# Layer norm moved from GpSimd to VectorE, together with six small moves in the order of work, in a fused attention and mixture-of-experts block

## The chip, the cores and the metric

The kernel runs on one core of a Trainium2 chip. The time is device microseconds of one execution. Before the change the median of three runs is 666.53 us (665.94 to 667.35).

## What is computed

```
x: (4, 512, 256)   ctx: (4, 1024, 192)   16 heads of 16, 8 experts, hidden 1024
x = x + tanh(g_xattn) * xattn(layernorm(x), ctx)
    q, k, v = linear(...)                        # with biases
    attn = softmax(clip(q k^T / 4, +-10000));    out = (attn v) @ Wo + bo
x = x + tanh(g_ffn) * ffn(layernorm(x))
    n = layernorm(x) * rsqrt(mean square + 1e-8) * norm_weight
    shared = relu(n @ sw1 + sb1) @ sw2 + sb2
    top 2 of 8 experts by sigmoid(n @ router^T), their weights made to sum to 1
    routed = sum over the two experts of weight * (relu(n @ ew1[e] + eb1[e]) @ ew2[e] + eb2[e])
    ffn = shared + routed
```

All tensors are fp32. Products keep fp32 accuracy by splitting each operand in a high and a low part and adding three matmuls (high-high, high-low, low-high).

## The kernel before, in words

Every engine has its own instruction list, and the lists meet at semaphores, so an instruction that waits holds up all that stands behind it on its engine. There are three stages.

**Preparation** (0 to 85 us). For each of the four batches n the list PREP (L388) gives the order of small steps, the same on TensorE (PE), ScalarE (ACT) and VectorE (DVE): TC, context transposes; K, Q, V, projections with halves or tiles j; TX, two transposes of the layer-normed x; N, checks on norms. In the batches 0 to 2 the second half of a batch is K2, K3, N0, V0, V1, N1, TX0, V2, TX1, V3; the last batch has the two TX ahead of K2. Eight PSUM banks are used in turn, so PE's step f waits for the DVE's step f-8. A batch's Q is made after the next batch's TC. ACT makes the high part of a step and DVE the low part. K and Q go out to DRAM through five stage buffers, and come back stacked by head: SP, the DMA queue, writes out step s and then starts up to three of batch 0's stack loads (L553 and the loop below it). The layer norm of batch n has three parts: statistics on DVE (`ln_x_stats`, L1096, at the step STATS_AT, just ahead of V2), the reciprocal root on GpSimd (POOL) and the subtract-and-scale of four tiles of 128 x 256, also on POOL (both in `norm_x`, L776). TX waits for it through the semaphore xn_done. The split of the weight wo is one DVE job (SPLIT_AT, L1318), ahead of TC0 of batch 1.

**Attention** (85 to 330 us). PE makes scores, ACT exponentials, PE the products with v in bank pv; DVE transposes each group's result out of pv and signals pv_read.

**Feed forward** (from 330 us), `feed_forward` on PE, ACT and DVE. The work is a list of chunks: chunks 0 to 4 are the shared expert on 256 tokens each; then 21 routed chunks in the order FFHFFFHFFHFFFHFFHFFHF, F of two tiles of tokens and H of one; then three shared ones. Each chunk has eight slots q: for two tiles PE does h0 to h3 (hidden layer, chunk i) and r0 to r3 (second layer of chunk i-1); for one tile the order is h0 h1 r0 h2 r1 h3 r2 r3, so that r0 of the chunk before comes after only two h. PE transposes the next chunk's input in slot `turn_at(i)` (L458), and DVE splits it there (`split_x`). ACT, at slot 0, first converts the next set's first weight (`w1_high`, 1 MB), and only then makes this chunk's relus, in order; DVE makes the low parts: `w1_low`, `split_h`(q) after each relu pair, `w2_low` at slot 6. A relu pair q waits for `split_h`(q-2), because its buffers are two. `w2_low` must end before r0 of this chunk, which stands in the next chunk. For an F chunk w1_low is in slot 0, but in slot 2 when the next chunk is H (there are six such places).

The last batch's remaining attention steps are put in between the shared chunks by LAST_AT (in eighths of a chunk, for PE) and LAST_READ (for DVE): the router's logits and top two at 18 on PE and 17 on DVE (`post`, `top_two`), the places of the tokens at 20 (`places`), which ends in the tile dest. POOL then scatters the rows of the tokens to slot_x in DRAM, and SP loads them by expert (`load_slot`). SP's list after that is written out by hand (L700): slot 0, w1(2), slot 1, biases(1), w2(1), then a loop over slot, w1, w2 and biases.

Of the kernel before, what the change touches and what calls it, by code (L numbers as in the profile page):

```python
# [27 lines left out]
def flamingo_block(nc, x, ctx_kv, g_xattn, g_ffn, wq, bq, wk, bk, wv, bv, wo, bo,  # L28
# [77 lines left out]
    with ExitStack() as top:  # L106
# [297 lines left out]
        FILLS = len(PREP)  # L404
        STATS_AT = (V, 2)
        STAGED = [(n, kind, j) for n, kind, j in PREP if kind in (Q, K)]
# [46 lines left out]
        X, EIGHTHS = "x", 8  # L453
        LAST_AT, LAST_READ = [3, 4, 16, 16, 18, 20], [3, 4, 16, 16, 17, 20]
        ZEROS_AT, LAST_NORM, SLOTS_AT = 10, 12, (20, 21)
        COMBINE_AT = [EIGHTHS * (AHEAD + MAIN) + k for k in COMBINE_E]

        def turn_at(i):  # L458

            return 6 if i == AHEAD - 1 else 4 if one_tile(i) else 2 if i == 0 or one_tile(i - 1) else 3  # L460

# [70 lines left out]
        def _(sp):  # L532
# [167 lines left out]
            load_slot(0)  # L700
            load_w1(2)
            load_slot(1)
            load_biases(1)
            load_w2(1)
            for j in range(MAIN):
                if j + 2 < MAIN:
                    load_slot(j + 2)
                if j + 3 < SETS:
                    load_w1(j + 3)
                load_w2(j + 2)  # L710
                load_biases(j + 2)
# [40 lines left out]
        def _(pool):  # L752
# [23 lines left out]
            def norm_x(n):  # L776
                wait_stats()
                rsqrt(0, mv[:, 0, :, 1], LN_EPS).then_inc(rstd_done, 1)
                pool.wait_ge(rstd_done, rounds[0])
                for t in range(QT):  # L780
                    last = nc.gpsimd.tensor_scalar(normed[:, n * QT + t, 0:D], x_sb[:, n * QT + t, :], mv[:, 0, t, 0:1],
                                                   rs[:, 0, t:t + 1], ALU.subtract, ALU.mult)
                    if t < QT - 1:
                        step(last)
                last.then_inc(xn_done, 1)

# [273 lines left out]
        def _(dve):  # L1060
# [35 lines left out]
            def ln_x_stats(n):  # L1096
                dve.wait_ge(loaded_x[n], 16)
                if n:
                    dve.wait_ge(xn_done, n)
                for t in range(QT):  # L1100
# [3 lines left out]
                last.then_inc(stats_done, 1)  # L1104
                stat_rounds[0] += 1

            def prep(f):
# [209 lines left out]

            SPLIT_AT = {(0, TC, 0): (W_K, wk_p), (0, K, 0): (W_V, wv_p), (0, K, 1): (W_Q, wq_p), (1, TC, 0): (W_O, wo_p)}  # L1318
            dve.wait_ge(ident_set, 1)
# [4 lines left out]
            for f, (n, kind, j) in enumerate(PREP):  # L1324
# [26 lines left out]
                if (n, kind, j) == (0, TC, 0):  # L1351
                    dve.wait_ge(loaded_bias, 80)
                    v.tensor_copy(bias_rows[0:2 * KD, :].rearrange("k (d q) -> k d q", q=PH),
                                  qk_rows[:, :].rearrange("k (q d) -> k d q", q=PH)).then_inc(bias_sorted, 1)
                if n + 1 < B and (kind, j) == STATS_AT:
                    ln_x_stats(n + 1)
# [253 lines left out]
            for i in range(len(CHUNKS)):  # L1610
                s = set_of(i)
                for q in range(EIGHTHS):
# [7 lines left out]
                    if at_e == LAST_NORM:  # L1620
                        norm_mlp(B - 1)
                    for k, when in enumerate(LAST_READ):
                        if when == at_e:
# [6 lines left out]
                    if q == turn_at(i) and i + 1 < len(CHUNKS):  # L1630
                        split_x(i + 1)
                    if CHUNKS[i][0] == F and q == (2 if one_tile(i + 1) else 0):
                        w1_low(s + 1)
# [54 lines left out]
        def _(pe):  # L1688
# [245 lines left out]
            def results(i, e):  # L1934

                s = set_of(i)
                if e == 0:
                    pe.wait_ge(w2_lo, s + 1)
                    pe.wait_ge(h_split, (i + 1) * HM // 2)
                    if i == 0:  # L1940
                        pe.wait_ge(pv_read, B * GROUPS)
                    if i >= 2:
# [15 lines left out]
            def feed_forward():  # L1958

                for i in range(len(CHUNKS)):  # L1960
                    for q in range(EIGHTHS):
# [71 lines left out]
```

## Time and profile before

| | us |
|---|---|
| median of the three runs | 666.53 |
| the profiled execution's own time | 665.94 |
| its span, first to last instruction | 664.2 |
| PE busy | 635.5 (96%) |
| ACT busy | 529.5 (80%) |
| DVE busy | 414.5 (62%) |
| POOL busy | 152.5 (23%) |

The span is 1.7 us shorter than the execution's own time. The page's PE count comes from modelled ends of pipelined matmuls, so that a busy PE is a PE with work in it, and its idle time is read from the gaps in the order of time. Times in the rows are in us from the span's start unless they are marked ns.

### The profile page before, as it was taken

Reading aid. Unit: us, or ns where it says so; the run is one execution under the profiler, and the core shown is the slowest. Engines: PE = TensorE matmul, PEld = TensorE weight load, DVE = VectorE, ACT = ScalarE, POOL = GpSimd, SP = SyncE. Lnnn points to the kernel's source line nnn. Section 1 sums busy time; section 2 is a strip of 40 time slices with the busy share of each in tenths; the row PEclk is TensorE's granted clock in tenths of the full one; section 3 lists DMA queues with packets and bytes.
Section 4 is the critical chain, followed back from the end, with each engine's and each line's share of the span. In section 5 each row is a group of like instructions: output and inputs, shape, how many; then the busy total and the mean of one; then the engine's idle time right before and its main releaser. Section 6 shows DMA issues by size and latency. Waiting matters only on the chain.

```text
span 664.2 us, 13111 instructions
## 1 busy us (share of the span) xinstructions
PE 635.5 (96%) x4733; PEld 451.1 (68%) x4733; DVE 414.5 (62%) x764; ACT 529.5 (80%) x852; POOL 152.5 (23%) x177
## 2 busy tenths in 40 slices
PE   5899989999999999999999999999999999999995
PEld 4678722223333323333399989999999999999995
DVE  5888710103434243434778867888797888888776
ACT  4577669999999899999873479687989979798850
POOL 3744260000403110410150400232222212314100
PEclk9999979999999999999999999999999999999998
DMA  7999900938398774943020896778878787894083
GB/s 249 301 327 287 376 20 1 130 53 104 78 237 160 131 91 54 121 91 124 10 64 1 195 299 223 250 235 256 259 245 285 240 257 249 259 284 161 29 277 125
DMA packets 75221, 118.52 MB, mean 178 GB/s; under 512 B 10933, under 2 KB 55945, under 8 KB 73993
## 3 DMA queue, kind: packets, MB, share of 16 engines
q1 hardware_dynamic: 66640, 102.38, 56.6%
q0 software_dynamic: 4416, 13.13, 7.0%
q10 hardware_dynamic: 4088, 2.05, 1.2%
q8 instruction: 41, 0.67, 0.5%
q14 instruction: 36, 0.29, 0.2%
HBM read 86.01 MB, written 31.52 MB: 177 GB/s over the span
## 4 chain that ended last, share of the span: by engine, by line
PE 49%; DVE 16%; ACT 12%; DMA 10%; issue 7%; POOL 2%; SPq 1%; ACTq 0%; POOLq 0%; DVEq 0%
PE pv L1824 19%; PE sc L1790 14%; PE sc L1695 5%; DMA b_sb<-in_L_ffn_eb 3%; ACT h_f L1018 3%; ACT h_p L1021 3%; ACT w_p L972 3%; DVE h_p L1546 3%; DVE w_p L1415 3%; PE pv L1950 2%; PE sc L1950 2%; DVE x_sb L1602 2%; PE mb L1695 2%; ACT w_p L978 2%; DMA slot_x<-second,dest 1%
## 5 line engine op out<-in xcount | busy, mean ns | idle before, releaser
L988 ACT ACTIVATE prob<-sc 128x1024 f32<-128x1024 f32 x172 | 169.2, 1180 | 11.5 <-PE sc L1790 11.5
L1018 ACT ACTIVATE h_f<-sc,b_sb 128x256 f32<-128x256 f32 (+1 forms) x232 | 94.0, 481 | 64.8 <-issue 22.6
L1695 PE MATMUL sc<-xt_p,w_p 128*128 128x256 f32 x1104 | 140.8, 284 | 2.6 <-DVE xt_p L1077 1.1
L1695 PEld LDWEIGHTS sc<-xt_p,w_p 128*128 128x128 f32 x1104 | 133.5, 190 | 5.7 <-DVE xt_p L1077 4.3
L1790 PEld LDWEIGHTS sc<-q_stack,k_stack 48*128 48x128 f32 x512 | 45.3, 186 | 114.0 <-ACT prob L988 62.4
L1790 PE MATMUL sc<-q_stack,k_stack 48*128 48x512 f32 x512 | 106.8, 476 | 2.9 <-ACT prob L988 2.2
L860 POOL DMA_INDIRECT y_tok<-y_sb,y_row x36 | 58.1, 1613 | 196.4 <-DVE y_sb L1566 191.8
L1021 ACT ACTIVATE h_p<-sc,b_sb 128x256 fp32r<-128x256 f32 (+1 forms) x232 | 95.4, 499 | 0.0
L1824 PE MATMUL pv<-prob,v 128*17 128x512 f32 x688 | 92.1, 608 | 0.2
L1546 DVE TENSOR_TENSOR h_p<-h_f,h_p 128x512 fp32r<-128x512 f32 x104 | 70.6, 687 | 34.2 <-ACT h_p L1021 34.1
L988 ACT ACTIVATE clip<-sc 128x1024 f32<-128x1024 f32 x84 | 88.0, 1183 | 1.7 <-PE sc L1790 1.7
L1950 PE MATMUL pv<-w_p,h_p 128*128 128x256 f32 x624 | 78.8, 284 | 0.3 <-issue 0.3
L1950 PE MATMUL sc<-w_p,h_p 128*128 128x256 f32 x624 | 78.2, 282 | 0.0
L1950 PEld LDWEIGHTS pv<-w_p,h_p 128*128 128x128 f32 x624 | 76.3, 191 | 0.8 <-issue 0.5
L1950 PEld LDWEIGHTS sc<-w_p,h_p 128*128 128x128 f32 x624 | 75.5, 189 | 0.5 <-DVE w_p L1420 0.4
L1375 DVE STREAM_TRANSPOSE o_q<-pv 128x512 f32<-128x512 f32 x16 | 11.5, 717 | 98.7 <-PE pv L1824 98.7
L1420 DVE TENSOR_TENSOR w_p<-w_raw,w_p 128x2048 fp32r<-128x2048 f32 x23 | 52.7, 2291 | 15.7 <-ACT w_p L978 15.7
L1415 DVE TENSOR_TENSOR w_p<-w_raw,w_p 128x2048 fp32r<-128x2048 f32 x23 | 52.7, 2289 | 1.9 <-ACT w_p L972 1.6
L972 ACT ACTIVATE w_p<-w_raw 128x2048 fp32r<-128x2048 f32 x22 | 43.0, 1955 | 11.0 <-DMA b_sb<-in_L_ffn_eb 10.4
L1824 PE MATMUL pv<-clip,v 128*17 128x512 f32 x336 | 44.2, 598 | 0.1
L978 ACT ACTIVATE w_p<-w_raw 128x2048 fp32r<-128x2048 f32 x22 | 43.8, 1991 | 0.0
L872 POOL DMA_INDIRECT slot_x<-normed,dest x16 | 16.4, 1028 | 115.6 <-DVE dest L1243 111.9
(271 smaller groups left out, 674.8 us busy)
## 6 DMA issues: line engine op xcount, KB each, us to landing
w_raw<-in_L_ffn_ew SPq DMA_DIRECT2D x42, 1024.0 KB, 6.5
k_stack<-k_rows SPq DMA_DIRECT2D x36, 256.0 KB, 10.4
k_rows<-stage_p SPq DMA_DIRECT2D x24, 256.0 KB, 4.4
q_stack<-q_rows SPq DMA_DIRECT2D x36, 128.0 KB, 11.5
y_tok<-zero_t POOLq DMA_DIRECT2D x8, 512.0 KB, 20.9
w_raw<-in_L_ffn_sw SPq DMA_DIRECT2D x4, 1024.0 KB, 7.6
y_all<-y_tok SPq DMA_DIRECT2D x8, 512.0 KB, 8.7
x_in<-slot_x SPq DMA_DIRECT2D x15, 257.0 KB, 2.8
```

The source lines that it names most:

```text
L860: pool.indirect_dma_start(out=y_tok, out_offset=bass.IndirectOffsetOnAxis(ap=y_row[i % 4][:, t:t + 1], axis=0), in_=y_sb[i % 2][:, t, :], ...
L972: nc.scalar.activation(w1_p[s % 2][0][:, :, :], w1_raw[s % 3], ACT.Copy).then_inc(w1_hi, 1)
L978: nc.scalar.activation(w2_p[s % 2][0][:, :, :], w2_raw[s % 2], ACT.Copy).then_inc(w2_hi, 1)
L988: nc.scalar.activation(prob_3[w % 3][u % 2][:, :, :], sc[u % 3][:, :, :], ACT.Exp, scale=SCALE).then_inc(exp_done, 1)
L1018: last = nc.scalar.activation(copy[:, m % len(ms), :], src[:, m % len(ms), :], ACT.Relu, bias=b1_sb[s % 3][:, m:m + 1])
L1021: last = nc.scalar.activation(high[:, m, :], src[:, m % len(ms), :], ACT.Relu, bias=b1_sb[s % 3][:, m:m + 1])
L1415: v.tensor_tensor(w1_p[s % 2][1][:, :, :], w1_raw[s % 3], w1_p[s % 2][0][:, :, :].bitcast(F32), ALU.subtract).then_inc(w1_lo, 1)
L1546: v.tensor_tensor(lo, src, hi.bitcast(F32), ALU.subtract).then_inc(h_split, 1)
L1695: last = mm(dst, lhs(a, k), rhs(b, k), start=(i == 0), stop=(i == len(todo) - 1))
L1790: return mm(dst[:, a, :], k_stack[rows, 2 * g + i, kt * P:(kt + 1) * P], q_stack[rows, 2 * g + i, :], start=True, stop=True)
L1824: last = mm(pv[32 * j:32 * j + DH + 1, :], v_sb[b][:, kt, HEADS // 2 * (j % 2) + 2 * g + j // 2, :], probs[w % len(probs)][j // 2][:, j % ...
L1950: last = mm(result_of(i, t), h_p[i % 2][a][:, k, t * P:(t + 1) * P], w2_p[s % 2][b][:, k, :], start=((k, a, b) == (0, 0, 0)), stop=((k, a, ...
```

## The change

The subtract-and-scale of the first layer norm goes from POOL to DVE as `ln_x`, ahead of K2 (of K0 in the last batch). The statistics come one step later, ahead of V3. The split of wo comes ahead of K3 of batch 0. DVE's logits step goes to 18, as on PE. slot_counts and slots go one eighth later. Chunk 4's turn of the next input goes from slot 6 to 5. SP's order after slot 0 becomes biases(1), w2(1), slot 1, w1(2). w1_low of every F chunk is in slot 0. PE waits for the last pv_read ahead of the first feed-forward product instead of ahead of the first second-layer product.

```diff
-        STATS_AT = (V, 2)
+        LN_AT, LN_LAST, STATS_AT = (K, 2), (K, 0), (V, 3)
-        LAST_AT, LAST_READ = [3, 4, 16, 16, 18, 20], [3, 4, 16, 16, 17, 20]
-        ZEROS_AT, LAST_NORM, SLOTS_AT = 10, 12, (20, 21)
+        LAST_AT = [3, 4, 16, 16, 18, 20]
+        ZEROS_AT, LAST_NORM, SLOTS_AT = 10, 12, (21, 22)
         def turn_at(i):
-            return 6 if i == AHEAD - 1 else 4 if one_tile(i) else 2 if i == 0 or one_tile(i - 1) else 3
+            return 5 if i == AHEAD - 1 else 4 if one_tile(i) else 2 if i == 0 or one_tile(i - 1) else 3
             load_slot(0)
-            load_w1(2)
-            load_slot(1)
             load_biases(1)
             load_w2(1)
+            load_slot(1)
+            load_w1(2)
                 # POOL, norm_x(n)
                 pool.wait_ge(rstd_done, rounds[0])
-                for t in range(QT):
-                    last = nc.gpsimd.tensor_scalar(normed[:, n * QT + t, 0:D], x_sb[:, n * QT + t, :], mv[:, 0, t, 0:1],
-                                                   rs[:, 0, t:t + 1], ALU.subtract, ALU.mult)
-                    if t < QT - 1:
-                        step(last)
-                last.then_inc(xn_done, 1)
                 # DVE, ln_x_stats(n)
-                if n:
-                    dve.wait_ge(xn_done, n)
+            def ln_x(n):
+                dve.wait_ge(rstd_done, stat_rounds[0])
+                for t in range(QT):
+                    last = v.tensor_scalar(normed[:, n * QT + t, 0:D], x_sb[:, n * QT + t, :], mv[:, 0, t, 0:1],
+                                           rs[:, 0, t:t + 1], ALU.subtract, ALU.mult)
+                    if t < QT - 1:
+                        step(last)
+                last.then_inc(xn_done, 1)
-            SPLIT_AT = {..., (1, TC, 0): (W_O, wo_p)}
+            SPLIT_AT = {..., (0, K, 3): (W_O, wo_p)}
+                if (kind, j) == (LN_LAST if n == B - 1 else LN_AT):
+                    ln_x(n)
-                    for k, when in enumerate(LAST_READ):
+                    for k, when in enumerate(LAST_AT):
-                    if CHUNKS[i][0] == F and q == (2 if one_tile(i + 1) else 0):
+                    if q == 0 and CHUNKS[i][0] == F:
                         w1_low(s + 1)
                 # PE, results(i, e)
-                    if i == 0:
-                        pe.wait_ge(pv_read, B * GROUPS)
             def feed_forward():
+                pe.wait_ge(pv_read, B * GROUPS)
```

## Rows read from the trace of the kernel before

**Rows 1.** Busy time by stretch: stretch, its length, busy time and count of each engine, clock, DMA.
```profile
0.00:86.00 86.00, 72.55 (x419) 60.55 (x419) 66.83 (x134) 50.31 (x86) 37.18 (x65) 1.00 0.90 299
...
460.00:627.00 167.00, 165.03 (x1331) 160.41 (x1330) 137.84 (x158) 143.32 (x287) 43.53 (x27) 1.00 0.73 234
```
**Rows 2.** Timeline, batch 0's layer norm: start, length, engine, line, operation, [idle before <- releaser].
```profile
19.64 5.20 POOL L781 TENSOR_SCALAR normed<-x_sb,mv,rs 128x256 f32<-128x256 f32 x4
...
24.98 0.63 PE L1721 MATMUL sc<-ident,normed 128*128 128x128 f32 x4 [2.65 <-POOL normed L781]
```
**Rows 3.** Timeline, the same operation on DVE in the second layer norm.
```profile
349.76 1.38 DVE L1309 TENSOR_SCALAR normed<-x_sb,mv,rs 128x256 f32<-128x256 f32 x4
```
**Rows 4.** DMA issues of 15.25 to 15.5 us (the last of wo): count, size, landing.
```profile
w_raw<-in_L_xattn_Wo SPq DMA_DIRECT2D x2, 32.0 KB, 8.3
```
**Rows 5.** Timeline of DVE, the split of wo.
```profile
30.79 0.42 DVE L1075 CAST wo_p<-w_raw 128x512 fp32r<-128x512 f32 x1
...
31.24 0.69 DVE L1077 TENSOR_TENSOR wo_p<-w_raw,wo_p 128x512 fp32r<-128x512 f32 x1
```
**Rows 6.** Timeline of DVE, SP and ACT in the batches 2 and 3.
```profile
57.54 0.75 DVE L1135 SCALAR_TENSOR_TENSOR stage_p<-sc,qk_col,stage_p 128x512 fp32r<-128x512 f32 x1 [0.40 <-ACT stage_p L948]
...
67.93 1.20 SPq L566 DMA_DIRECT2D q_rows<-stage_p  x2
...
78.70 0.69 ACT L947 ACTIVATE stage_s<-sc,qk_col 128x512 fp32r<-128x512 f32 x1 [0.75 <-DMA k_rows<-stage_p]
```
**Rows 7.** Timeline, start of the feed-forward stage.
```profile
330.38 3.14 PE L1695 MATMUL sc<-xt_p,w_p 128*128 128x256 f32 x24
...
330.51 0.72 DVE L1375 STREAM_TRANSPOSE o_q<-pv 128x512 f32<-128x512 f32 x1 [0.20 <-PE pv L1824]
...
334.41 0.84 ACT L1018 ACTIVATE h_f<-sc,b_sb 128x256 f32<-128x256 f32 x2 [5.47 <-DMA b_sb<-in_L_ffn_sb]
```
**Rows 8.** Timeline of DVE from the logits to the places.
```profile
357.74 0.31 DVE L1187 STREAM_TRANSPOSE logits<-sc 128x128 f32<-128x128 f32 x1
...
360.78 1.28 DVE L1546 TENSOR_TENSOR h_p<-h_f,h_p 128x512 fp32r<-128x512 f32 x2
...
366.22 0.17 DVE L1243 CAST dest<-dest_f 128x8 uint32<-128x8 f32 x1
```
**Rows 9.** Chain of waits, the first routed input: start, length, what.
```profile
385.64 2.65 DMA x_in<-slot_x
```
**Rows 10.** Timeline of PE, first products of chunks 5 and 6.
```profile
392.93 4.48 PE L1695 MATMUL sc<-xt_p,w_p 128*128 128x256 f32 x36 [1.01 <-issue]
...
404.82 4.48 PE L1695 MATMUL sc<-xt_p,w_p 128*128 128x256 f32 x36
```
**Rows 11.** Timeline of SP, the load of w2(1).
```profile
390.70 0.38 SPq L662 DMA_DIRECT2D w_raw<-in_L_ffn_ew  x1
```
**Rows 12.** DMA issues of 390.6 to 391.1 us.
```profile
w_raw<-in_L_ffn_ew SPq DMA_DIRECT2D x1, 1024.0 KB, 5.9
```
**Rows 13.** Timeline of ACT, DVE and PE, chunks 5 to 7.
```profile
393.64 1.92 ACT L972 ACTIVATE w_p<-w_raw 128x2048 fp32r<-128x2048 f32 x1 [4.33 <-DMA b_sb<-in_L_ffn_eb]
...
415.86 2.28 DVE L1420 TENSOR_TENSOR w_p<-w_raw,w_p 128x2048 fp32r<-128x2048 f32 x1
...
419.21 1.60 PE L1950 MATMUL pv<-w_p,h_p 128*128 128x256 f32 x12
```
**Rows 14.** Timeline of DVE, ACT and PE, chunk 13 and the H chunk behind it.
```profile
484.76 0.69 DVE L1546 TENSOR_TENSOR h_p<-h_f,h_p 128x512 fp32r<-128x512 f32 x1 [0.70 <-ACT h_p L1021]
...
485.89 0.96 ACT L1018 ACTIVATE h_f<-sc,b_sb 128x256 f32<-128x256 f32 x2
...
491.01 2.28 DVE L1420 TENSOR_TENSOR w_p<-w_raw,w_p 128x2048 fp32r<-128x2048 f32 x1
...
493.40 1.63 PE L1950 MATMUL sc<-w_p,h_p 128*128 128x256 f32 x12
```
**Rows 15.** Timeline of ACT, an F chunk whose w1_low is in slot 0.
```profile
444.02 0.84 ACT L1018 ACTIVATE h_f<-sc,b_sb 128x256 f32<-128x256 f32 x2 [0.97 <-DVE h_p L1546]
```

More of the change, by code:

```diff
@@ L1314, in norm_mlp @@
                                 ALU.mult).then_inc(normed_done, 1)
-            SPLIT_AT = {(0, TC, 0): (W_K, wk_p), (0, K, 0): (W_V, wv_p), (0, K, 1): (W_Q, wq_p), (1, TC, 0): (W_O, wo_p)}
+            SPLIT_AT = {(0, TC, 0): (W_K, wk_p), (0, K, 0): (W_V, wv_p), (0, K, 1): (W_Q, wq_p), (0, K, 3): (W_O, wo_p)}
             dve.wait_ge(ident_set, 1)
```

## The prediction, made before the changed kernel was run

> **What bounds the kernel.** I read the busy time by stretch first, then the order of time of each engine at every place that the diff touches, then the waits and the DMA landings there. In the routed part PE works 165 of 167 us, so what makes PE late there is seldom given back; DVE has 138 and ACT 143 us of work in the same 167, in strict order, and so the question at each place is whether a moved step comes too late for PE. In the preparation DVE has 67 of 86 us and PE 73 [rows 1]. The attention stage in between is passed through whole: a shift at its start is a shift at its end.
>
> **Layer norm on DVE.** POOL takes 5.2 us for the four tiles, and PE stood idle 2.65 us for them in batch 0 [rows 2]. DVE takes 1.38 us for the same four in the second layer norm [rows 3]. Ahead of K2 of batch 0 DVE would end it near 21.2, so the PE wait of rows 2 goes. What is late next is DVE itself. The last piece of wo, issued at 15.4, lands 8.3 us later, at 23.7 [rows 4], while DVE is now at its split before K3, near 21.9: it waits 1.8 us, and the split takes 0.42 + 0.69 = 1.1 [rows 5]. K3, N0, V0, V1, N1 and TX0 queue behind it, and so PE's banks. I get DVE's split of TX1, for which Q waits, at 29.9 instead of 30.3, and then the statistics (2.2 us, now behind it) make the splits of the next TC about 0.9 later than before. ACT, which is full at K0 and K1 of batch 1, takes that up. So the gain of 2.65 is gone by batch 1.
>
> In the batches 1 and 2 the 1.38 us comes on DVE between K1 and K2, where it waited 0.40 for ACT before each K [rows 6]; two such gaps hide 0.8 and 0.6 stays. TX1 comes earlier than before in its batch, since the statistics are behind it, and spares PE short waits for Q, but the TC splits after it are 0.6 later, and with them Q of batch 2, whose write holds SP. SP starts that pair of writes at 67.93 and issues back to back from there up to the write of K0 [rows 6]; ACT waits at 78.70 for the landing of that write. All later steps to the first scores hang on it: **+0.6 us**. The bounds: -2.3 if wo costs nothing and the earlier Q is kept by PE, +1.5 if DVE's whole 1.38 counts. I take 0.6 as what the order of time gives. The x tiles wanted by bo come no later. On POOL only the copies of ctx follow, and they come earlier.
>
> The Trainium skill speaks against the move ("Perfetto Trace Analysis", Optimizing Scalar/DVE Operations): with DVE saturated, moving work off it, even to GPSIMD, may make sense. The trace agrees only in part, with 67 of 86 us. By that rule alone, an estimate with the duration of the rows, 1.38 us would be paid in full in each of the three later batches, 4.1 us instead of 0.6.
> It also says where the two meet ("SBUF — State Buffer", Who interferes with whom): VectorE and GpSimd share one port pair, and whoever comes second blocks for the whole instruction; a tensor_scalar from SBUF to SBUF can take the pair. No row of the kernel before shows this operation beside a POOL copy. By that rule the copies of ctx, which now follow the root at once, could hold back ln_x in two batches; one block would be under a microsecond, and it is in no term of the sum.
>
> **Wait for pv_read ahead of feed_forward.** PE starts the first product at 330.38, DVE's last transposition runs 330.51 to 331.23 [rows 7]. PE starts 0.9 later, and h0 to h3 and the two wo steps are queued behind. But ACT's first relu waits for the biases until 334.41 [rows 7], with h0 ready at 332 before and 333 now, and PE waited later on for a split of DVE's that hangs on that relu. **0**, and 0.9 if this cover were gone.
>
> **Logits on DVE at 18.** At 17 DVE took the logits at 357.74 and did chunk 2's second and third split_h together at 360.78, 3.0 us later [rows 8]. Now the second split comes first. Its relus end near 358.5, the split takes 0.7, so the logits start at 359.2, 1.5 later. PE's places wait for the masks 2.4 us on, 361.7 instead of 360.75: PE stands 1.0. On DVE one split fewer follows, so that dest, at 366.22 before, comes 1.0 later. From dest the path goes through POOL's eight scatters to the first routed input, landing at 388.3 [rows 9]. **+1.0**, bounds 0 and 1.5. The shift of slot_counts and slots changes no neighbour on DVE (there is nothing in those slots of chunk 2): 0.
>
> **Turn of the first routed input in slot 5.** PE gets to it after r0, waits until 389.3 for the landing, and has 0.4 of transposes and r1 to r3, 36 matmuls in 4.3 us, to do after it: 394.1. Before, chunk 5 began at 392.93, with 1.0 of waiting for w1_low [rows 10]. Against 393.9 by the last step alone, **+0.2**, bounds 0 and 1.5 (r1 alone).
>
> **SP's order.** The new place of w1(2) is the issue at 390.7, which was w2(1)'s and landed 5.9 us later, at 396.6, with the same bytes ahead of it [rows 11, 12]. ACT waited until 393.64 (for the biases, which were behind w1(2)) [rows 13]. It converts w1(2) before it makes a relu of chunk 5, so it starts 3.0 later; w1_low, the splits and the input of chunk 6 queue behind it. With the 1.0 of above: w1_high ends 399.6, w1_low 401.9, the first split 402.5, the third relu pair 404.0, its split 404.6, the input's split 406.1. PE wants it at 404.82 + 1.2 = 406.0 [rows 10]. So +0.2 there. ACT then runs relus, w2(1) and w1(3) to 409.2. DVE has w2_low (409.6), two steps of read_y (411.0), w1_low(3) (413.3), two splits, the input, the expert weights (419.3), w2_low (421.6). It began this last one at 415.86 and ended it 1.07 us ahead of PE's r0 at 419.21 [rows 13]. PE now wants it at 420.6 and waits 1.0. **+1.2**, bounds -0.3 (the biases come early) and +3.0 (all of it).
>
> **w1_low in slot 0 before an H chunk.** Its 2.29 us now stands ahead of the first split_h, for which ACT's third relu pair waits. Where that order is in the trace already, ACT idles 0.97 us for the split [rows 15]. At chunk 13 DVE is free at 484.06, waits 0.70 for ACT and splits at 484.76, and ACT's third pair begins at 485.89 unhindered [rows 14]. Now: w1_low to 486.3, split to 487.0, third pair 1.1 later, and so w2_high; w2_low, which began at 491.01 as soon as DVE was free, begins near 491.8 and ends at 494.1. PE began r0 at 493.40, with only the two h of an H chunk as cover [rows 14]: +0.7. Of six such places three are like this (I work out 0.7, 0.85 and 0.6); in the other three w2_low ends 1 us or more ahead of r0, as in rows 13. **+2.2**, bounds -0.4 (the input's split comes earlier) and six times 1.1, 6.6.
>
> **Sum.** 0.6 + 1.0 + 0.2 + 1.2 + 2.2 = 5.2. On the profiled execution's own 665.94 (span 664.2 and 1.7 around it) that is **671.1**. That execution is 0.6 below the median of the three, so by the median it would be 671.7; I keep 671.1.
>
> **Rivals.**
> *The stretch before the scores decides (faster).* PE's 2.65 us wait goes and is not replaced: wo has landed or its split is hidden, Q of batch 0 starts 2.3 earlier and all to the end is carried along; the other edits fall into slack. For it: POOL's chain is on the chain of waits there. Against it: 8.3 us to landing [rows 4]. It decides if DVE's TX1 split of batch 0 ends before 28.5. Time 665.9 - 2.3 = 663.6. Chance 0.1.
> *Only the dispatch counts.* The losses in routed chunks fall on waits that PE has anyway, or earlier input splits give them back: 0.6 + 1.2 = 1.8, 667.7. For it: PE idles about 2 us in that part [rows 1]. Against it: r0 behind an H's two h has no cover. Chance 0.2.
> *Every H place pays.* Three more at 0.9: 5.2 + 2.7, 673.8. For it: later w2_low holds back SP's next load. Against it: slack of rows 13. Chance 0.1.
> *The forecast*: 0.6, its own range 668.5 to 673.5.
>
> **Numbers.** The range 666.8 to 674.2 leaves out the faster case and a little at the top. Taking 0.2% (1.3 us, about what a measurement of this kernel can tell from no change) around 666.5: the faster case gives 0.1, the second case half its 0.2 for no change, the rest slower: 0.1, 0.1, 0.8.
>
> **What would show it.** In the profile after: DVE idle or waiting for wo at about 22 to 24; no PE wait for normed in batch 0, and first scores 0.6 later; dest 1.0 later relative to the last product with v; ACT waiting for a w_raw load near 397; ACT idle for split_h in the third pair of the chunks before H; PE waiting for w2_low ahead of r0 in H chunks. The forecast fails if the first scores come 2 us earlier, or if w2_low of chunks 13, 20 and 23 still ends ahead of r0.

## The result, and the profile of the changed kernel

The changed kernel takes 675.1 us (median of 4, 673.48 to 675.87), the kernel before beside it 666.94 us: a ratio of 1.0116, 95% interval 1.0088 to 1.0145, 8 us slower. The forecast of 671.1 us (666.8 to 674.2) had the sign and missed the size. A later set of runs of both gave 1.0086 (1.0056 to 1.0116).

The profiled execution of the changed kernel takes 674.95 us; its span is 673.2 us, where that of the kernel before was 664.2. I lay the same PE instructions of both traces side by side. How much later than before:

| place | changed kernel later by, us | forecast |
|---|---|---|
| first score | 2.32 | 0.6 |
| turn of the first routed input | 3.31 | 1.6 |
| turn in chunk 5 (second routed input) | 3.51 | 1.8 |
| turn in chunk 6 | 5.56 | 2.0 |
| turn in the first H chunk | 6.45 | 3.0 |
| last routed input | 9.11 | 5.2 |

By these offsets the preparation lost 2.3 us (forecast 0.6), the dispatch and the turn 1.2 (1.2), SP's order 2.9 (1.2), and w1_low in slot 0 2.7 (2.2).

Stretches of the changed kernel, columns as in [rows 1]:
```profile
0.00:86.00 86.00, 71.27 (x411) 60.01 (x411) 69.16 (x143) 50.45 (x86) 16.69 (x48) 0.96 0.90 299
...
460.00:627.00 167.00, 162.89 (x1307) 157.72 (x1306) 136.33 (x157) 140.23 (x280) 55.49 (x28) 1.00 0.75 243
```
The norm left POOL (37.2 to 16.7 us in the first 86). DVE has only 2.3 us more in these 86, because the stage is longer now; up to the first score of each kernel it has 69.7 us where it had 65.3. The last column but two is the granted clock: 0.96 in place of 1.00 in the preparation.

DVE in batch 0, the place of [rows 2, 4, 5]:
```profile
19.90 1.51 DVE L1102 TENSOR_SCALAR normed<-x_sb,mv,rs 128x256 f32<-128x256 f32 x4
...
24.94 0.43 DVE L1069 CAST wo_p<-w_raw 128x512 fp32r<-128x512 f32 x1 [2.88 <-DMA w_raw<-in_L_xattn_Wo]
25.40 0.69 DVE L1071 TENSOR_TENSOR wo_p<-w_raw,wo_p 128x512 fp32r<-128x512 f32 x1
26.01 0.75 DVE L1136 SCALAR_TENSOR_TENSOR stage_p<-mb,qk_col,stage_p 128x512 fp32r<-128x512 f32 x1
```
Its PE:
```profile
21.55 0.63 PE L1724 MATMUL sc<-ident,normed 128*128 128x128 f32 x4 [0.29 <-DVE normed L1102]
...
26.81 1.01 PE L1750 MATMUL mb<-wv_p,ctx_p 128*128 128x256 f32 x3 [2.99 <-DVE stage_p L1136]
...
29.11 2.23 PE L1733 MATMUL sc<-ident,ctx_raw 128*128 128x128 f32 x16
31.10 3.00 PE L1698 MATMUL sc<-xn_p,wq_p 128*128 128x512 f32 x12
35.10 0.93 PE L1744 MATMUL pv<-ctx_p,wk_p 128*128 128x512 f32 x3 [1.01 <-DVE ctx_x L1120]
```
and the stretch of that wait:
```profile
25.00:30.00 5.00, 3.19 (x16) 3.19 (x17) 4.97 (x9) 0.00 (x0) 0.61 (x1) 0.66 0.96 347
```
PE's wait for the norm went from 2.65 to 0.29 us. In its place DVE stands 2.88 us for wo with K3's bank behind it, and PE 2.99 us for that bank. After that idle time the granted clock is 0.66 in the stretch, so part of it ran at 1.2 GHz: the three products with wv_p take 1.01 us, in [rows 2]'s batch at full clock 0.52 to 0.60.

The start of the routed part; the answers to [rows 9 to 13]. SP (slot 0, slot 1, w1(2)):
```profile
388.96 0.39 SPq L681 DMA_DIRECT2D x_in<-slot_x  x1
...
392.89 0.38 SPq L681 DMA_DIRECT2D x_in<-slot_x  x1
394.03 0.64 SPq L652 DMA_DIRECT2D w_raw<-in_L_ffn_ew  x1
```
The chain of waits from it:
```profile
394.03 7.42 DMA w_raw<-in_L_ffn_ew
401.52 1.93 ACT w_p L966
403.54 2.29 DVE w_p L1418
```
PE there:
```profile
391.74 0.63 PE L1867 MATMUL sc<-ident,x_in 128*128 128x128 f32 x4 [1.88 <-DMA x_in<-slot_x]
...
396.52 4.41 PE L1698 MATMUL sc<-xt_p,w_p 128*128 128x256 f32 x36
...
410.27 4.58 PE L1698 MATMUL sc<-xt_p,w_p 128*128 128x256 f32 x36 [1.77 <-DVE xt_p L1071]
...
425.56 1.69 PE L1951 MATMUL pv<-w_p,h_p 128*128 128x256 f32 x12 [0.64 <-DVE w_p L1423]
```
w1(2) lands 7.4 us after its issue; ACT begins it 5.0 us after the first routed product (0.7 in [rows 10, 13]), and the lateness comes out at chunk 6's input (1.77) and the first H chunk's weights (0.64).

PE's first second-layer products of chunks 13, 20 and 23, the answers to [rows 14]:
```profile
500.74 1.68 PE L1951 MATMUL sc<-w_p,h_p 128*128 128x256 f32 x12 [0.99 <-DVE w_p L1423]
...
575.85 1.70 PE L1951 MATMUL pv<-w_p,h_p 128*128 128x256 f32 x12 [0.98 <-DVE w_p L1423]
...
607.97 1.68 PE L1951 MATMUL sc<-w_p,h_p 128*128 128x256 f32 x12 [0.99 <-DVE w_p L1423]
```
ACT waits 0.96 us for split_h in the third relu pair of chunk 13, as in [rows 15]:
```profile
493.53 0.84 ACT L1012 ACTIVATE h_f<-sc,b_sb 128x256 f32<-128x256 f32 x2 [0.96 <-DVE h_p L1549]
```

### The profile page after: what moved, and what is told of

Its sections match the earlier page's. It is cut to its first block, busy times and chain, and to the rows that moved or that the text cites. A ratio compares the mean times of both kernels' runs of the same rounds, so it can differ in the third digit from the quotient of the medians.

```text
span 673.2 us, 13111 instructions
## 1 busy us (share of the span) xinstructions
PE 637.5 (95%) x4733; PEld 451.6 (67%) x4733; DVE 419.2 (62%) x780; ACT 529.7 (79%) x852; POOL 145.8 (22%) x161
## 4 chain that ended last, share of the span: by engine, by line
PE 47%; DVE 18%; ACT 14%; issue 9%; DMA 6%; SPq 3%; POOL 1%; ACTq 0%; POOLq 0%; DVEq 0%
PE pv L1827 19%; PE sc L1793 14%; DVE w_p L1418 4%; PE sc L1698 4%; ACT h_f L1012 3%; ACT h_p L1015 3%; ACT w_p L966 3%; PE pv L1951 2%; SPq L534 2%; DVE h_p L1549 2%; ACT w_p L972 2%; PE sc L1951 2%; DVE x_sb L1605 2%; PE mb L1698 1%; DVE w_p L1423 1%
## 5 line engine op out<-in xcount | busy, mean ns | idle before, releaser
L854 POOL DMA_INDIRECT y_tok<-y_sb,y_row x36 | 70.8, 1968 | 189.5 <-DVE y_sb L1569 184.9
L1549 DVE TENSOR_TENSOR h_p<-h_f,h_p 128x512 fp32r<-128x512 f32 x104 | 70.1, 687 | 31.0 <-ACT h_p L1015 30.9
```

Of the source, the lines that this page charges most:

```text
L854: pool.indirect_dma_start(out=y_tok, out_offset=bass.IndirectOffsetOnAxis(ap=y_row[i % 4][:, t:t + 1], axis=0), in_=y_sb[i % 2][:, t, :], ...
L1549: v.tensor_tensor(lo, src, hi.bitcast(F32), ALU.subtract).then_inc(h_split, 1)
```

## The experiments

Ratios are to the kernel before in the same set of runs, with 95% intervals. The sets differ: in most the kernel before took 667.7 to 668.7 us, in those marked * 679.6. The record has the number 1 for the chip of a set of either kind, so it doesn't show that the chip makes this difference. Past the first score, traces of * aren't laid beside the one of the kernel before. Offsets and waits are of single profiled executions. "Theory A" and the like are the rival outcomes put on record ahead of each run.

### One step undone in the changed kernel

**SP's order.**
```diff
             load_slot(0)
+            load_w1(2)
+            load_slot(1)
             load_biases(1)
             load_w2(1)
-            load_slot(1)
-            load_w1(2)
```


> The changed kernel with SP's old order after slot 0 (w1(2), slot 1, biases(1), w2(1)) and nothing else undone. Theory A (the two traces side by side): w1(2), issued at 394.0 behind the slot-1 load and landing 7.4 us later, keeps ACT waiting until 401.5, and the lateness is handed on by DVE to the input of chunk 6 (1.9 us) and to the weights of the first H chunk (0.9 us); so the time falls by 2.75 us from 675.1 to about 672.4, ACT's first routed relu or w1_high starts within 1 us of the first routed product instead of 5 us after it, and chunk 6 starts 3.6 to 3.9 us later than in the kernel before. Theory B (my prediction's size, 1.2 us): 673.9. Theory C: the step at chunk 6 comes from the logits and the turn, and the order of SP is hidden: 675.


Ratio 1.0044 (1.0027 to 1.0062). ACT begins 1.5 us after the first routed product and PE has no wait at chunk 6: between the turns in chunk 5 and the first H chunk 0.02 us are lost, 2.94 before the undoing. Theory A in the path that it names. In size it missed: ACT starts 1.5 us behind the product and not within 1, chunk 6 is 2.0 us later than before and not 3.6 to 3.9, and the median fell further than 2.75.

**w1_low.**
```diff
-                    if q == 0 and CHUNKS[i][0] == F:
+                    if CHUNKS[i][0] == F and q == (2 if one_tile(i + 1) else 0):
```


> The changed kernel with w1_low in slot 2 again ahead of H chunks, nothing else undone. Theory A: the three r0 of H chunks 13, 20 and 23 that now wait about 1 us for w2_low stop waiting; the time falls by 2.6 us to about 672.5, and the offset against the kernel before stays constant from chunk 8 to the end. Theory B: what those three places lose is carried in from the later start of the routed part, so the waits for w2_low stay or turn into others: 674.5 to 675.


Ratio 1.0073 (1.0048 to 1.0099). The three waits are gone, and the offset is 6.69 us at the first H chunk and 6.65 at the last routed input. Theory A.

**wo.**
```diff
-            SPLIT_AT = {..., (0, K, 3): (W_O, wo_p)}
+            SPLIT_AT = {..., (1, TC, 0): (W_O, wo_p)}
```


> The changed kernel with wo's split again ahead of TC0 of batch 1, nothing else undone; the layer norm stays on DVE. Theory A: DVE's wait of 2.9 us for wo at 22 to 25 us goes, PE's wait of 3.0 us for a bank at 26.8 goes and with it the half clock that followed, and Q of batch 0 starts about 28.2 instead of 31.1; if all is carried on, the first score comes at about 84 (2.3 to 2.9 earlier), 672.5. Theory B: DVE's 1.38 us in each batch and the statistics behind it decide, not wo: the gain in batch 0 is lost by batch 2, the first score stays at 86 or later, 674.5 to 675. Theory C (in between): the split of wo, 1.1 us, comes back in the place where DVE is full: 673.5.


Ratio 1.0047 (1.0032 to 1.0063). The first score comes 0.80 us before that of the kernel before, where the two runs above, on the same chip, have it 2.2 and 2.0 after. Theory A: wo costs about 3 us, and the norm is no loss. All traces on record say the same: with the norm on DVE and wo at K3 after its late loads, the first score is 1.6 to 2.9 us later than in the trace of the kernel before (five traces), and with wo at TC0 of batch 1 it is between 1.95 earlier and 0.9 later (eight).

**The whole again.**


> The changed kernel once more, beside the single steps and on their chip, as the sum to hold the steps against. Theory A: the steps add up: -0.5% (norm), +0.55% (wo), +0.45% (SP's order), +0.3% (w1_low), +0.1% (logits and turn), so 1.009 to 1.012. Theory B: they amplify each other: alone they sum to clearly less than the whole.


Ratio 1.0086. With the first runs that is about 1.010; against it the undone steps are worth 0.57% (SP), 0.28% (w1_low) and 0.54% (wo), each give or take some 0.3%, so that w1_low by itself isn't told from nothing here. These three and the norm's gain of 0.5% (below) add up to about the whole, as in theory A. The steps added one by one to the norm (below) do not: -0.50, +0.46 (wo), +0.27 (w1_low), +0.09 (SP) and +0.12 (logits and turn) make +0.44%, as in theory B, and nearly all of the gap is SP's order.
Here the wait at chunk 6 is as long as in the first trace, but the 36 products after it take 6.07 us in place of 4.58, and the clock is 0.55:
```profile
409.26 6.07 PE L1698 MATMUL sc<-xt_p,w_p 128*128 128x256 f32 x36 [1.78 <-DVE xt_p L1071]
```
```profile
411.00:414.00 3.00, 3.00 (x17) 3.00 (x17) 2.96 (x3) 2.79 (x6) 0.00 (x0) 0.55 0.84 277
```
The same in e2_w1low_back (wait 2.01, then 6.07). So a wait of about 2 us there costs 2 or 3.5.

### The norm alone, and one step added to it

**The norm alone.** The changed kernel with SP's order, w1_low, wo, logits and turn as before.


> Only the layer norm on DVE with its statistics ahead of V3, and the wait for pv_read at the start of the stage; wo's split, the logits, the turn, SP's order and w1_low are as in the kernel before. Theory A: the norm on DVE by itself costs nothing or gains what PE waited for POOL in batch 0 (2.65 us), so 664.5 to 667. Theory B: DVE pays its 1.38 us in the later batches and in the last batch ahead of K0: 668 to 669.


Ratio 0.9950 (0.9933 to 0.9966): faster, 3.3 us. Theory A. PE in batch 0:
```profile
22.07 0.63 PE L1724 MATMUL sc<-ident,normed 128*128 128x128 f32 x4 [1.45 <-DVE normed L1102]
...
27.56 3.00 PE L1698 MATMUL sc<-xn_p,wq_p 128*128 128x512 f32 x12 [0.30 <-DVE xn_p L1116]
32.66 0.93 PE L1744 MATMUL pv<-ctx_p,wk_p 128*128 128x512 f32 x3 [2.10 <-DVE ctx_x L1120]
```
```profile
25.00:30.00 5.00, 4.70 (x32) 4.05 (x31) 4.86 (x14) 3.88 (x8) 0.90 (x3) 1.00 1.09 365
```
Q starts 2.86 us earlier than before; 2.1 go again at K0 of batch 1, where DVE has the statistics and wo's split in a row; the first score is 1.56 earlier in this trace. The clock stays at 1.00.

**Plus wo at K3.**


> As e7_only_ln with wo's split ahead of K3 of batch 0 and nothing else of the change (wo's loads where they were). Undoing this alone in the changed kernel gave back 0.7% or 4.6 us. Theory A: wo's late landing is the mis-sized term: done alone it costs 3 to 4 us over e7_only_ln, ratio 0.9995 to 1.001, with DVE waiting 2.5 to 3 us for wo and PE 3 us for its bank. Theory B: the other steps of the change amplify it: alone under 2 us, 0.998 or lower.


Ratio 0.9996 (0.9983 to 1.0010), 0.46% above the norm alone. DVE and PE:
```profile
25.24 0.43 DVE L1069 CAST wo_p<-w_raw 128x512 fp32r<-128x512 f32 x1 [2.96 <-DMA w_raw<-in_L_xattn_Wo]
```
```profile
27.11 0.86 PE L1750 MATMUL mb<-wv_p,ctx_p 128*128 128x256 f32 x3 [3.08 <-DVE stage_p L1136]
```
```profile
25.00:30.00 5.00, 2.89 (x14) 2.89 (x15) 4.73 (x9) 0.05 (x1) 0.62 (x1) 0.73 1.02 374
```
Theory A: wo at K3 costs 3 us by itself, with the same wait and a fall of the clock (0.73).

**Plus wo at K3, its loads issued ahead of the x tiles of batches 1 to 3.***
```diff
+            wo_rows = wo.rearrange("(a k g i d) n -> g i a d k n", a=2, k=KD, g=2, i=2)
+            for j in range(4):
+                ...
             for n in range(1, B):
                 load(x_sb[:, n * QT:(n + 1) * QT, :], x_t[n], loaded_x[n])
-            wo_rows = ...
```


> As e7_only_ln, with wo's split ahead of K3 of batch 0 as in the changed kernel, but wo's eight loads issued ahead of the x tiles of batches 1 to 3. Theory A: what costs is the landing of wo, not the place of the split; with the loads issued 4 us earlier DVE doesn't wait (under 0.5 us) and PE's wait of 3.0 us at 26.8 is gone: within 0.7 us of e7_only_ln, 664 to 665.5. Theory B: the 1.1 us of the split itself ahead of K3 hold the banks: PE stands 1 us or more, 666 or later. Theory C: the queues are full, wo lands after 22 all the same, and 666.5 to 668.


Ratio 0.9943 (0.9916 to 0.9970). DVE:
```profile
21.75 0.74 DVE L1136 SCALAR_TENSOR_TENSOR stage_p<-pv,qk_col,stage_p 128x512 fp32r<-128x512 f32 x1
22.41 0.41 DVE L1069 CAST wo_p<-w_raw 128x512 fp32r<-128x512 f32 x1
```
No wait, the clock of 25 to 30 us at 1.00, and the whole loss gone. It was the landing, not the place of the split. The split's own 1.1 us does show in that place, at Q of batch 0, but K0 of batch 1 starts where it does with the norm alone (32.56 and 32.66):
```profile
28.52 2.99 PE L1698 MATMUL sc<-xn_p,wq_p 128*128 128x512 f32 x12 [1.05 <-DVE xn_p L1116]
```

**wo at K3, the norm on POOL.*** One entry of SPLIT_AT in the kernel before.


> The kernel before with wo's split ahead of K3 of batch 0; the norm stays on POOL. Theory A: DVE waits for wo's landing whoever makes the norm, about 4 us from 20.5 to 24.5, but PE waits for POOL until 25 at the same time, so most is hidden: first score 0.5 to 1.5 us later than before, 667.5 to 669. Theory B: the cost is of wo alone and independent of the norm: the whole 3.1 us seen between the changed kernel and e3_wo_back, 670.5.


Ratio 1.0010 (0.9982 to 1.0038). DVE waits as long, but PE waits for POOL at the same time:
```profile
24.49 0.43 DVE L1075 CAST wo_p<-w_raw 128x512 fp32r<-128x512 f32 x1 [3.20 <-DMA w_raw<-in_L_xattn_Wo]
```
```profile
25.99 0.63 PE L1721 MATMUL sc<-ident,normed 128*128 128x128 f32 x4 [4.04 <-POOL normed L781]
```
By the ratio theory A: B's 3.1 us, 0.46%, lie above the interval. PE never waits for K3's bank; POOL's lateness covers DVE's. The trace is worse than A's forecast all the same (first score 3.65 us later than before, not 0.5 to 1.5): POOL begins its four tiles at 20.39 in place of 19.64, and the clock falls to 0.67 (25 to 30 us) behind the wait of 4.04.

**Plus w1_low.**


> As e7_only_ln, with w1_low in slot 0 for every F chunk and SP's order as in the kernel before. Theory A: the cost of w1_low ahead of H chunks is its own, 0.7 to 0.9 us at chunks 13, 20 and 23, 2.5 us together: ratio to before 0.9988. Theory B: it came only because SP's order had made the routed part late; alone it costs under 0.5 us: 0.9955. Theory C: without the other changes it also shows at the first H chunk and costs over 3.3 us: 1.000.


Ratio 0.9977 (0.9960 to 0.9993), 0.27% above the norm alone; PE waits at the same three places, 1.01, 0.98 and 0.98 us, and the trace loses 2.7 us over them. Theory A.

**Plus SP's order of the change.**


> As e7_only_ln with SP's order of the changed kernel (biases(1), w2(1), slot 1, w1(2)) and nothing else. Theory A: 2.7 to 3.3 us, ratio 0.9995: ACT gets w1(2) 7 to 8 us later than in the kernel before, and the steps at chunk 6 and at the first H chunk add up to about 2.9. Theory B: without the later logits the first routed chunk has more room: under 1.5 us, 0.997. Theory C (from e12_sp_third, where slot 1 as the fourth made PE wait 0.59 us): the slot-1 load as the third costs some of it at the turn of the second routed chunk.


Ratio 0.9959 (0.9946 to 0.9972), 0.09% above the norm alone, not told from none.
```profile
396.81 1.92 ACT L966 ACTIVATE w_p<-w_raw 128x2048 fp32r<-128x2048 f32 x1 [8.03 <-DMA w_raw<-in_L_ffn_ew]
```
```profile
392.35 4.34 PE L1698 MATMUL sc<-xt_p,w_p 128*128 128x256 f32 x36 [1.01 <-issue]
405.57 4.58 PE L1698 MATMUL sc<-xt_p,w_p 128*128 128x256 f32 x36 [1.31 <-DVE xt_p L1071]
```
w1(2), issued at 390.18, is begun 6.6 us later, 4.5 after the first routed product; in the changed kernel, its repeat, e2 and e3 it is 7.5 to 7.8 and 5.0 to 5.3. Lost between the turns: 1.8 here, 2.9 there. The trace is between A and B, the ratio below both. At the first H chunk PE has no wait here, and 0.2 us are lost from the turn before it; in the changed kernel it is 0.9, with the wait of 0.64. The other step at work there is w1_low, which in the changed kernel stands ahead of chunk 6's splits too. With w1_low moved and SP's order as before (e1_sp_back, e13_w1low_only) nothing is lost at that chunk; with both moved e3_wo_back shows the wait again, 0.66 (e18_after_again, where PE loses 3.5 us just before, has none). So some 0.7 us of the 2.9 come only when both steps meet.

**biases(1) first, then w1(2), slot 1, w2(1).***


> As e7_only_ln, with SP's order after slot 0: biases(1), w1(2), slot 1, w2(1). Theory A: it is w1(2) being the fourth that costs in the changed kernel; with it second the routed part keeps pace and the earlier biases give ACT's first relu nothing, since w1_high comes ahead: 664.3 to 665. Theory B: any change of this order that delays w1(2) costs at chunk 6, here by about the time of two issues (1.1 us): 665.7. Theory C: w2(1), the last, becomes late for r0 of chunk 5: PE waits for w2_low there, 666 or more.


Ratio 0.9956 (0.9934 to 0.9979), and 0.0 us between the turns. Theory A.

**w1(2) third, slot 1 fourth.**


> As e7_only_ln, with SP's order after slot 0: biases(1), w2(1), w1(2), slot 1, so that w1(2) is third and slot 1 fourth. With w1(2) second (e11_bias_first) nothing was lost at chunk 6, with it fourth (the changed kernel) 2.9 us were. Theory A: what costs is how late ACT gets w1(2): third, it is issued some 1.1 us earlier than in the changed kernel and lands 1 to 1.5 us earlier, so the step between the turns of chunks 5 and 7 is 1 to 2 us instead of 2.9; ratio to before about 0.9975. Theory B: it is the slot-1 load's place that counts: now fourth, it costs as much or more, 0.9995 or slower. Theory C: the chain has slack up to third place: 0.995.


Ratio 0.9953 (0.9937 to 0.9969). Lost from the first turn to the one in the H chunk: 1.3 us, of them 0.59 a wait of PE for slot 1's input and 0.7 behind the turn in chunk 5, where theory A has 1 to 2:
```profile
398.62 0.63 PE L1867 MATMUL mb<-ident,x_in 128*128 128x128 f32 x4 [0.59 <-DMA x_in<-slot_x]
```
No theory fits whole, and the ratio is C's: counted from the first turn, second, third and fourth place lose 0, 1.3 and 1.7 us in the traces, while in the medians no step of this series is seen.

**Plus logits at 18 and turn in slot 5.***


> As e7_only_ln (the norm on DVE, wo's split, SP's order and w1_low as before), with the logits of DVE at 18 and the turn in slot 5 as in the changed kernel. Theory A (my prediction's terms): the masks come 1.0 us later for PE's places and the turn costs 0.2, so it is 1.2 us slower than e7_only_ln: 665.8 (ratio to before 0.997), and PE waits 0.8 to 1.0 us for the masks. Theory B: waits behind it take this up: 664.6 (0.995). Theory C: the 1.4 us that e7_only_ln gained between the first shared product and the routed input came from exactly this, so it is more than 1.2: 667 (0.999).


Ratio 0.9962 (0.9936 to 0.9988). PE waits for the masks as forecast, but the end isn't told from the 0.9956 and 0.9943 of the same set. Open between A and B.
```profile
364.41 0.38 PE L1779 MATMUL sc<-mask_s,before 128*128 128x32 f32 x2 [0.87 <-DVE mask_s L1212]
```

**The same plus SP's order.***


> The changed kernel with wo's split at TC0 of batch 1 and w1_low in slot 2 ahead of H chunks again: the norm on DVE, the logits at 18, the turn in slot 5 and SP's new order stay. Without SP's order this is e8_logits_turn (0.9962 on its chip), without logits and turn it is e17_sp_only (0.9959; 1.8 us between the turns of chunks 5 and 7). Theory A: the earlier turn lets PE begin chunk 5 sooner after the slot-0 load, and so the same late w1(2) costs it more: 2.4 to 3 us between the turns, more where the clock falls in the wait, ratio 1.000 to 1.002. Theory B: SP's order costs the same 1.8 us with or without the turn, and what amplified it in the whole was w1_low: ratio 0.998.


Ratio 0.9963 (0.9948 to 0.9978), against 0.9962 without SP's order (another set): no loss, neither theory. In this set PE comes late to the routed part for another reason. PE before it:
```profile
379.40 0.27 PE L1951 MATMUL pv<-w_p,h_p 128*128 128x256 f32 x1 [1.15 <-issue]
380.12 0.48 PE L1951 MATMUL pv<-w_p,h_p 128*128 128x256 f32 x1 [0.45 <-issue]
381.53 0.37 PE L1951 MATMUL pv<-w_p,h_p 128*128 128x256 f32 x1 [0.94 <-issue]
```
PE waits between single products for nothing that the profile shows, then runs with the clock at 0.66 (380 to 390 us), and so comes to the routed input when it has landed: it turns that input 6.6 us after SP issues its load (2.8 in the changed kernel's first trace), there is no wait for x_in, and ACT begins w1(2) 1.2 us after the first routed product instead of 5.0. What these waits are the trace doesn't say. So whether the turn amplifies SP's order stays open.

### Where the gain of the norm is eaten

**Only batch 0's norm on DVE**, those of batches 1 to 3 on POOL, in the kernel before.
```diff
+                if (n, kind, j) == (0, K, 2):
+                    ln_x(0)
```


> The kernel before, with only batch 0's subtract-and-scale on DVE (ahead of K2) and those of the batches 1 to 3 on POOL; the statistics stay ahead of V2. Theory A: DVE's 1.38 us in each later batch are what ate the 3.0 us gained in batch 0, so here more of it reaches the first score: 2.3 to 3.0 us earlier than before, ratio 0.996 or lower, and below that of e7_only_ln in the preparation. Theory B: the 3.0 us end at ACT and DVE around the context transposes of batch 1 whatever batches 1 to 3 do: first score 1 to 1.7 us earlier, as in e7_only_ln. Theory C: with the statistics ahead of V2 POOL's 5.2 us are again late for a later batch's TX: no gain.


Ratio 0.9942 (0.9921 to 0.9962), not told from the norm alone; Q of batch 0 now waits 2.41 us for TX1's split behind the statistics, so only 1.0 us of the gain reaches Q, which then takes 4.57 us in place of the 3.00 of full clock (granted 0.66 from 29 to 34 us). The first score is 0.4 us earlier than before, less than either A or B has, though the ratio is in A's range:
```profile
29.38 4.57 PE L1708 MATMUL sc<-xn_p,wq_p 128*128 128x512 f32 x12 [2.41 <-DVE xn_p L1126]
```
**Statistics of batches 1 and 2 ahead of their own K1.**
```diff
-                if n + 1 < B and (kind, j) == STATS_AT:
+                if n == B - 2 and (kind, j) == STATS_AT:
+                    ...
+                if 0 < n < B - 1 and (kind, j) == (K, 1):
+                    ln_x_stats(n)
```


> As e7_only_ln, but the statistics of batches 1 and 2 ahead of their own K1 and their ln_x ahead of N0, instead of ahead of the V3 of the batch before and K2. Theory A: PE's wait of 2.1 us for the context splits of batch 1 (DVE is busy with 2.2 us of statistics and the split of wo just ahead of them) goes, and the first score comes 1 to 2 us earlier than in e7_only_ln; ratio 0.992 to 0.9935. Theory B: DVE's 2.2 us only move to K1, where the banks are held as long: same as e7_only_ln, 0.995. Theory C: POOL's root comes late for ln_x: slower, over 0.997.


Ratio 0.9973 (0.9956 to 0.9990). K0's wait of 2.1 us is gone, but TX0 of batches 1 and 2 waits 1.76 and 1.66 us for the norm. The ratio is theory C's, its cause isn't: POOL's root has ended when DVE comes to ln_x (39.4 and 40.4 us in batch 1), and the norm is late by its place in DVE's order.

**wo's split at K1 of batch 1.**


> As e7_only_ln with wo's split at K1 of batch 1 instead of TC0 of batch 1. Theory A: ahead of TC0 its 1.1 us is part of PE's wait of 2.1 us for the context splits of batch 1; at K1 it falls on DVE's waits for ACT (0.4 to 1.3 us before each K): that PE wait becomes 1.0 and the first score comes 0.5 to 1 us earlier: ratio 0.994. Theory B: ACT is full there, the shift is lost again before the scores: 0.995. Theory C: SP's stack loads wait for the split and the last batch's rows come later: 0.996 or more.


Ratio 0.9943 (0.9924 to 0.9963). K0's wait falls from 2.10 to 1.03, and N1 of batch 1 waits 1.32 for ACT; the first score is 1.2 us later than before, not earlier. A and B are not told apart by the ratio.

**Both: batch 0's norm on DVE, batch 1's statistics ahead of V3, wo at K1.***


> The kernel before with only batch 0's subtract-and-scale on DVE, batch 1's statistics ahead of V3 of batch 0 (those of batches 2 and 3 ahead of V2), and wo's split at K1 of batch 1. Theory A: the wait of 2.4 us for xn_p at batch 0's Q (e14_ln0_on_dve, statistics ahead of TX1's split) goes and the context splits of batch 1 are not held by wo: first score 1 us earlier than in e14_ln0_on_dve, ratio 0.992 to 0.994. Theory B: ACT and the writes of the staged rows set the pace from batch 1 on: 0.994 to 0.996 as before. Theory C: POOL's 5.2 us for batch 1, now begun 2 us later, are late for TX0 of batch 1: 0.997 or more.


Ratio 0.9938 (0.9914 to 0.9962), the lowest, and inside the intervals of the norm alone, e10_wo_early, e14_ln0_on_dve and e19_wo_later. The interval holds A's range and B's; in the trace the first score is 1.8 us earlier than in e14_ln0_on_dve, more than A's 1. A version faster than the kernel before by 0.5 to 0.6% exists; which of these is best isn't settled.

## Why the prediction was too low, step by step

- **Layer norm on DVE, +0.6: the step that failed**, with wo in it. I saw the 8.3 us to landing and DVE's wait (1.8 forecast, 2.88 measured: the last load was issued at 17.3 in place of 15.4 and landed at 24.9; nothing ahead of these loads was changed, but the end of their issues moves from 15.8 to 18.7 us between the traces), and wrote that ACT takes up the lateness, "so the gain of 2.65 is gone by batch 1". It was more than gone. I followed DVE's steps to TX1's split (forecast 29.9, measured 30.9, by the landing's 1.2), and never asked when the bank of K3 comes free for PE: that wait is 2.99 us, the slow clock behind it takes about another 1.1 (the products and transposes between the wait and Q take 4.3 us, in the kernel before 3.2), and K0 of batch 1 begins 1.7 later where I had it even. From there to the first score another 0.6 is lost, as forecast, though one trace can't confirm a term so small. The term was +0.6 and came out at 2.3. Without wo in the way the norm gains 0.5% in time (e7_only_ln; the seven other runs with it in which wo isn't late for its split and w1_low and the statistics aren't moved lie between 0.9943 and 0.9963), so the forecast's lower bound ("if wo costs nothing") was the case without wo, and the upper one, +1.5, left out PE's wait for the bank.
- **The rule on a saturated DVE** (the Trainium skill, "Perfetto Trace Analysis", Optimizing Scalar/DVE Operations) speaks against the move, and the prediction worked out 4.1 us from it; the norm alone made the kernel faster by 0.5%. With 67 of 86 us busy, DVE isn't the saturated engine of that rule. The four tiles take 1.51 us beside a copy on POOL and 1.36 without, so the port pair that VectorE and GpSimd share (the Trainium skill, "SBUF — State Buffer", Who interferes with whom) costs 0.15 us here at most.
- **pv_read, 0**: PE waited 0.84 us, and nothing was left of it later: e17_sp_only has the same wait, and PE's next wait, for the split of the wo step, is 0.33 us in place of 1.37.
- **Logits, +1.0, and turn, +0.2**: the mask wait is 0.88 us, and the first routed product is 1.3 later than before relative to the first score. From the first feed-forward product to the first routed one the five traces with both steps take 62.3 to 63.0 us, and e7_only_ln, e13_w1low_only, e16_wo_k3_only and e17_sp_only, without them, 61.1 to 61.5: some 1.4 us. In the sets marked * the traces don't show it (68.0 us in e8_logits_turn, 67.9 in e11_bias_first). Right in the traces of the other sets; too small for the medians to confirm.
- **SP's order, +1.2: mis-sized, 2.9.** The chain was the forecast one. Its first term was 5.9 us to landing, from [rows 12]; the load took 7.4 from the same place, so ACT was 5.0 us behind PE's first routed product and not 3.5, and the loss is greater by about as much. The bytes ahead are the same, as the prediction says, but the 1 MB load before this one is now issued 2.3 us ahead of it (391.75 and 394.03) where it was 3.9 (386.80 and 390.70), so more of it can be in flight. That this is the cause is argued and not shown: e17_sp_only has the same 2.3 and its landing took 6.6, the other four traces 7.4 to 7.7. The rest of the difference is the first H chunk, where w1_low adds to it: the prediction priced the two steps apart. Undone in the whole the order gives 0.57%, added alone 0.09%. In the traces it is 2.9 to 3.8 against 1.8; longer landing, w1_low at the first H chunk and, in two of five traces, the slower clock behind the wait at chunk 6 make up that difference, but no run takes them apart in the medians.
- **w1_low, +2.2**: 2.7 in the trace, nearly all at the three chunks named, 0.9, 0.9 and 0.8 us; 0.27 to 0.28% both ways, about 1.9 us. Right, but for the meeting with SP's order.
- **Range**: its top, 674.2, took no account of the clock. Behind the new wait for K3's bank (2.2 to 3.4 us) the clock fell in all five traces that have it (0.66 to 0.83 from 25 to 30 us), behind the one at chunk 6 (1.3 to 2.1) in two of five, and that comes on top of the wait.

The rival "the stretch before the scores decides" named the right condition (wo landed or hidden) and was refused for the right row. With wo's loads early its first half comes true (DVE's TX1 split ends near 28.4 and the kernel is 0.57% faster, e10_wo_early). Its second half, that the other edits fall into slack, doesn't: w1_low costs 0.27% beside the norm alone.

## What to carry to other kernels

When an instruction that waits for a DMA is moved earlier, follow not only the engine that waits but the buffer that it holds: ask which bank or tile is released behind it and who stands for it, and price that in full, also where the wait removed just ahead of it seems to pay. Give a landing time taken from a row a third of error: here a load of 1 MB with the same bytes ahead of it landed after 5.9 us in one trace and 6.6 to 7.7 in five others. Take a bundle apart before rejecting it: here one part was a gain of 0.5%, hidden under 1.5% of losses.

## What the runs showed of the hardware

- A PE wait of 1.8 us at the same instruction was followed by full clock in one execution and by 0.55 in another (part of the stretch at 1.2 GHz), 36 products taking 4.58 or 6.07 us. The kernel before had a wait of 2.65 us and kept 1.00.
- The kernel before took 668 us in some sets of runs and 679.6 in others. All six traces of the latter have PE waits of 0.34 to 1.15 us on "issue" between single matmuls at 377 to 387 us, and take 250.1 to 251.2 us from the first score to the first feed-forward product, where the others take 245.8 to 247.0; there SP's order cost nothing (e20_sp_with_turn).
- Profiles of one and the same preparation differ: with the norm alone the first score came 1.56 us before that of the kernel before in one trace, and with only w1_low added, which the preparation doesn't see, 0.90 after. In the eight traces that share it, it lies between 1.95 before and 0.90 after. In this stage a term under some 2.5 us can't be read from one pair of traces; between places closer together, as in the routed part, smaller ones repeat.
